# Softmax sums of the row mixing: four reciprocals replaced by a logarithm, an exponential and one correcting step

## The reference, cut to what matters

```
def _L0_xattn_ref(q, k, v, gamma):
    h = N_HEAD                         # 8 heads of 32 rows in each of 8 batches
    qk = jnp.einsum('bhdq,bhdl->bhql', qh, kh) * scale
    sm = jax.nn.softmax(qk, axis=-1)
    ret = jnp.einsum('bhql,bhdl->bhdq', sm, vh)
    ...
    return gamma * ret
x = x + _L0_xattn_ref(_layernorm(x), ctx_2048, ctx_2048, L0_xattn_gamma)
```

## Time and profile before

| what | value |
| --- | --- |
| median of three runs | 1866.02 us |
| profiled execution | 1868.98 us, span 1867.2 us |
| PE busy over the span | 91% |
| DVE, ACT, POOL busy over the span | 80%, 67%, 49% |
| row mixing | from the start to about 361 us of the span |
| one step with unpacking | 19.83 us |
| one step without unpacking | 19.60 us |

### The profile page before, as it was taken

How to read it: one execution, slowest core, us unless ns; L and a number is a source line. 1 busy time by engine, 2 the same in 40 slices (tenths; PEclk the granted TensorE clock), 3 DMA queues, 4 the chain that set the end, 5 groups by cost and what they waited for, 6 DMA issues and landing times. The chain is left out here.

```text
span 1867.2 us, 30272 instructions
## 1 busy us (share of the span) xinstructions
PE 1699.0 (91%) x10553; PEld 747.7 (40%) x10706; DVE 1494.4 (80%) x2799; ACT 1248.7 (67%) x2107; POOL 907.1 (49%) x927
## 2 busy tenths in 40 slices
PE   3999999689999977989799999999999997999999
PEld 0333233134444433434244444444444444444444
DVE  5899999876867664877699999999999995884332
ACT  4888888445544431223399999999999995774333
POOL 5667665355445420000088888888888884000000
PEclk8999999889999998999899999999999998999999
DMA  9856551301011005556455555655666667110220
GB/s 203 224 147 139 143 145 29 105 11 23 1 23 23 1 6 175 101 101 116 89 108 108 109 109 108 113 109 114 114 114 106 105 108 229 31 23 27 42 45 23
DMA packets 421687, 170.45 MB, mean 91 GB/s; under 512 B 382112, under 2 KB 392352, under 8 KB 420384
## 3 DMA queue, kind: packets, MB, share of 16 engines
q1 hardware_dynamic: 421536, 168.51, 41.8%
HBM read 69.89 MB, written 4.19 MB: 40 GB/s over the span
## 5 line engine op out<-in xcount | busy, mean ns | idle before, releaser
L1586 ACT ACTIVATE a_prob<-a_psS,a_bias,q_scale 128x1024 uint8<-128x1024 f32 x512 | 610.7, 1210 | 25.5 <-PE a_psS L1479 20.5
L1515 DVE TENSOR_REDUCE a_tops<-a_psM 128x1 f32<-128x512 f32 x1024 | 622.7, 681 | 2.0 <-PE a_psM L1469 0.6
L1565 POOL CAST a_wide<-a_pairs 128x2048 int16<-128x2048 uint8 x256 | 481.4, 1891 | 96.9 <-DMA a_pairs<-a_prob 87.8
L1469 PE MATMUL a_psM<-KT,QO 128*128 128x512 bf16 x969 | 354.0, 387 | 21.9 <-DVE a_tops L1515 10.5
L1479 PE MATMUL a_psS<-KT,QO 128*128 128x512 bf16 x966 | 292.6, 380 | 6.7 <-ACT a_prob L1586 3.7
L1491 PEld LDWEIGHTS a_psO<-V,a_wide 128*128 128x128 f16 x4096 | 174.9, 96 | 144.9 <-DVE QO L1528 23.0
L1491 PE MATMUL a_psO<-V,a_wide 128*128 128x32 bf16 x4096 | 181.3, 177 | 20.4 <-DVE QO L1528 15.6
L843 DVE SCALAR_TENSOR_TENSOR g_sum<-g_psG,gu_scale,g_sum 128x512 f32<-128x512 f32 x176 | 124.2, 746 | 89.8 <-PE g_psG L995 75.0
L821 POOL TENSOR_TENSOR g_sum<-g_sum 128x512 f32<-128x512 f32 x88 | 126.3, 1435 | 140.4 <-DVE g_sum L843 140.4
L478 ACT ACTIVATE prob<-psT 128x512 f32<-128x512 f32 x256 | 142.9, 599 | 63.8 <-remote 32.0
L942 ACT ACTIVATE g_sum<-g_psG,gu_scale 128x512 f32<-128x512 f32 x176 | 111.2, 681 | 109.9 <-PE g_psG L995 109.0
(11 more groups left out here) (212 smaller groups left out, 2737.5 us busy)
## 6 DMA issues: line engine op xcount, KB each, us to landing
xs<-in_x SPq DMA_DIRECT2D x64, 256.0 KB, 6.2
cs<-in_ctx SPq DMA_DIRECT2D x64, 256.0 KB, 8.3
KT<-in_w SPq DMA_DIRECT2D x2, 4096.0 KB, 19.1
raw_gu<-in_gu SPq DMA_DIRECT2D x4, 1408.0 KB, 8.1
vs<-in_ctxT SPq DMA_DIRECT2D x16, 256.0 KB, 2.9
QO<-in_ctxT SPq DMA_DIRECT2D x4, 1024.0 KB, 11.3
a_pairs<-a_prob SPq DMA_TRANSPOSE x256, 2.7
out<-x_sb SPq DMA_DIRECT2D x16, 256.0 KB, 2.2
```

Of the source, the lines that this page charges most:

```text
L1469: pe.matmul(psM[n % NM][:, :], QOf[:, i * P:(i + 1) * P], KTf[:, keys:keys + 512], start=True, stop=True).then_inc(shown, 1)
L1515: v.reduce_max(tops[i // JOIN % NB][:, i % JOIN, c:c + 1], psM[n % NM][:, :], AX.X).then_inc(topped, 1)
L1565: pool.tensor_copy(wide[i % NV][:, :, :, :].rearrange("p k c q -> p k (c q)"), both).then_inc(widened, 1)
L1586: act.activation(prob[i % NP][:, k * HK:(k + 1) * HK], psS[g % NS][:, :], ACT.Exp, scale=q_scale[:, i:i + 1], bias=bias[i // JOIN % NB][:, ...
```

## The change

The four reciprocals of 128 columns on VectorE go. In their place ScalarE computes the logarithm of the sums straight from PSUM and then the exponential of its negative, which gives an approximate reciprocal r of the whole 512 columns. One correcting step follows: with the sum s, r is improved to r(2 - s r). VectorE computes -s r into e_sums (scalar_tensor_tensor), and then (2 - s r) times weighed (a second scalar_tensor_tensor); GpSimd's product with r is what it was. ScalarE's four instructions of `collect` are spread over n = 0, 1, 2 and 4, where the two of before stood at n = 0. VectorE's two stand at n = 8 and 11, where its four stood at 5, 8, 11 and 14. TensorE's weighed sums of the next tile wait for three reads of psO and psE, where they waited for two.

```diff
-    INVERT, STATS = (5, 8, 11, 14), (2, 13)
+    COLLECT, INVERT, STATS = (0, 1, 2, 4), (8, 11), (2, 13)
@@ GpSimd, finish(j)
-                pool.wait_ge(inverted, HT * (j + 1))
-                pool.tensor_tensor(weighed[j % 2][:, :], weighed[j % 2][:, :], rinv[:, :],
+                pool.wait_ge(inverted, j + 1)
+                pool.tensor_tensor(weighed[j % 2][:, :], weighed[j % 2][:, :], rinv[j % 2][:, :],
@@ ScalarE
-            def collect(j):
+            def collect(j, i):
...
-                act.activation(weighed[b][:, :], psO[:, :], ACT.Copy, scale=gamma[:, :]).then_inc(o_read, 1)
-                act.activation(e_sums[b][:, :], psE[:, :], ACT.Copy).then_inc(o_read, 1)
+                if i == 0:
...
+                    act.activation(weighed[b][:, :], psO[:, :], ACT.Copy, scale=gamma[:, :]).then_inc(o_read, 1)
+                if i == 1:
+                    act.activation(e_sums[b][:, :], psE[:, :], ACT.Copy).then_inc(o_read, 1)
+                if i == 2:
+                    if j:
+                        act.wait_ge(rinv_ready, j)
+                    act.activation(logs[:, :], psE[:, :], ACT.Ln).then_inc(o_read, 1)
+                if i == 3:
+                    act.wait_ge(o_read, 3 * (j + 1))
+                    act.activation(rinv[b][:, :], logs[:, :], ACT.Exp, scale=-1.0).then_inc(rinv_ready, 1)
@@ VectorE
-            def invert(j, h):
...
-                at = slice(h * P, (h + 1) * P)
-                v.reciprocal(rinv[:, at], e_sums[j % 2][:, at]).then_inc(inverted, 1)
+            def invert(j, i):
+                b = j % 2
+                if i == 0:
+                    v.wait_ge(rinv_ready, j + 1)
+                    v.scalar_tensor_tensor(out=e_sums[b][:, :], in0=e_sums[b][:, :], scalar=-1.0, in1=rinv[b][:, :],
+                                           op0=ALU.mult, op1=ALU.mult).then_inc(corrected, 1)
+                if i == 1:
+                    v.wait_ge(corrected, j + 1)
+                    v.scalar_tensor_tensor(out=weighed[b][:, :], in0=e_sums[b][:, :], scalar=2.0,
+                                           in1=weighed[b][:, :], op0=ALU.add, op1=ALU.mult).then_inc(inverted, 1)
@@ TensorE, weigh(j, 0)
-                        pe.wait_ge(o_read, 2 * j)
+                        pe.wait_ge(o_read, 3 * j)
```

More of the change, by code:

```diff
@@ L260, in mix_rows @@
         e_sums = [sb(f"e_sums{i}", [P, DM], F32) for i in range(2)]
-        rinv = sb("rinv", [P, DM], F32)
+        logs = sb("logs", [P, DM], F32)
+        rinv = [sb(f"rinv{i}", [P, DM], F32) for i in range(2)]
         psS = [pb(f"psS{i}", [P, DM], F32) for i in range(3)]
@@ L275, in mix_rows @@
         tscored, exped, pv_done, o_read = (sem(f"m_{n}") for n in ("tscored", "exped", "pv_done", "o_read"))
+        rinv_ready, corrected = sem("m_rinv"), sem("m_corrected")
         inverted, mixed_s, added, after_s, bits_s = (
@@ L479, in exp @@
                                scale=float(D0) ** -0.5).then_inc(exped, 1)
-            def collect(j):
+            def collect(j, i):
                 b = j % 2
[L484 to L487, removed]
-                act.activation(weighed[b][:, :], psO[:, :], ACT.Copy, scale=gamma[:, :]).then_inc(o_read, 1)
-                act.activation(e_sums[b][:, :], psE[:, :], ACT.Copy).then_inc(o_read, 1)
+                if i == 0:
+                    act.wait_ge(pv_done, NU * (j + 1))
+                    if j >= 2:
+                        act.wait_ge(mixed_s, j - 1)
+                        act.wait_ge(added, j - 1)
+                    act.activation(weighed[b][:, :], psO[:, :], ACT.Copy, scale=gamma[:, :]).then_inc(o_read, 1)
[8 more added lines that the diff above has]
+                    act.activation(rinv[b][:, :], logs[:, :], ACT.Exp, scale=-1.0).then_inc(rinv_ready, 1)
             def first_high(k):
@@ L501, in steps @@
                         exp(j, n)
-                    if n == 0 and has(j - 1):
-                        collect(j - 1)
+                    if n in COLLECT and has(j - 1):
+                        collect(j - 1, COLLECT.index(n))
                     if has(j + 2):
@@ L517, in _ @@
             turns(steps)
-            collect(NT - 1)
+            for i in range(len(COLLECT)):
+                collect(NT - 1, i)
         @block.vector
@@ L654, in _ @@
             turns(steps)
-            for h in range(HT):
-                invert(NT - 1, h)
+            for i in range(len(INVERT)):
+                invert(NT - 1, i)
             after(NT - 2)
```

## The result

The changed kernel takes 1871.68 us (median of 9 runs, 1869.71 to 1873.92), the kernel before 1865.41 us in the same comparison (9 runs, 1863.23 to 1867.11). The ratio is 1.0033, 95% interval 1.0023 to 1.0043: slower by 0.33%, or 6.3 us, although VectorE (DVE) has less to do: 1477.3 us busy instead of 1494.4. ScalarE (ACT) rose from 1248.7 to 1264.2. The profiled execution took 1871.7 us, with a span of 1869.9 us and a mean granted clock of 0.98.

The account below looks back on a forecast made before the run. PE's own work plus three short waits for DVE bound a step. Steps 3 to 13 +6.6, steps 1 and 2 +0.8, step 14 -0.26, step 15 +0.4, tail -2.65: +4.9, giving 1870.9 us; range 1867 to 1876.

Parts of the forecast that it names:

- Of the reciprocals only the one at n = 8 counts at the sixteenth score: PE's wait for the sixteenth score: one of four removed reciprocals counts, gaining 0.26 us if its replacement starts on time.
- The first new instruction is held by the keys: DVE's first scalar_tensor_tensor waits for GpSimd's keys until 10.7; sixteenth score at 12.0 instead of 11.86, 0.14 us lost.
- Queries later, unpacking and second new instruction held, split late: GpSimd's queries start at 12.7 and delay DVE; PE's turning of the maxima at 16.7, 0.6 us a step lost.
- Which hold costs how much: Steps with unpacking: DVE's new instructions wait for GpSimd's keys and queries, losing 0.6 us a step.
- Steps 1 and 2 at +0.4 each: Row mixing steps without unpacking: turning of the maxima at 16.25 instead of 15.86, together +0.8 us.
- Step 13 counted as one more of 0.6: Last of steps 3 to 13, each taken to lose 0.6 us, 11 times, +6.6 us.
- Step 14 at -0.26: Row mixing step in which GpSimd makes no keys or queries: 0.26 us gained.
- Step 15 at +0.4: Row mixing step without scores: the logarithm stands in the chain of exponentials PE follows, 0.4 us lost.
- tail at -2.65: End of the row mixing: the shorter chain starts GpSimd's last product at 355.15 instead of 357.81, 2.65 us gained.
- not held: Rival: DVE's new instructions never wait for GpSimd; 0.46 us gained in 11 steps, together -8.1, 1857.9; chance 0.17.
- only the first hold: Rival: only DVE's first new instruction waits for GpSimd; 0.0 a step, tail gain remains, -2, 1864; chance 0.17.
- ScalarE takes over: Rival: logarithm and exponential cost 0.8 each, delaying exponentials and queries; 0.3 a step more, +9, 1875; chance 0.08.

Follow-up runs that it names:

- Experiment 3: Kernel before with its four reciprocals kept; ScalarE's logarithm and exponential added as in the changed kernel, result unused: 1869.39 us, ratio 1.001 to the kernel before.
- Experiment 4: Changed kernel with the second scalar_tensor_tensor moved behind the split (n = 14), the first left at n = 8: 1863.33 us, ratio 0.9978 to the kernel before.
- experiment 1: Changed kernel with both scalar_tensor_tensor replaced by one-input statistics instructions, correcting step left out: 1862.68 us, ratio 0.9971 to the kernel before.

## Why the prediction held, step by step

It said 1870.9 and slower by 4.9 us; the medians say 1871.7 and 6.3. That the two times lie within 0.8 is in part luck: the change was 1.4 larger than the sum, and the kernel before 0.6 faster in the second comparison (1865.41 against 1866.02).

- *Of the reciprocals only the one at n = 8 counts at the sixteenth score.* Held for the one at n = 5: the three maxima behind it start at 8.42 in both profiles, and in the changed one DVE sits idle 0.93 ahead of them (210.70). DVE's busy time in the window of 200 to 220 us fell from 19.63 to 18.04, and the step got longer. The one at n = 11 stood right ahead of the split, so it did lie on PE's path, by at most the wait of 0.17 there; the working has it in the instants, but not in that sentence.
- *The first new instruction is held by the keys.* Held: keys to 10.74 (10.7 said), instruction 1.07 long (about 1.1 said), score at 12.04 (12.0). PE's wait there grew from 0.81 to 0.99 (near 0.9 said).
- *Queries later, unpacking and second new instruction held, split late.* Held: queries at 12.77 (12.7), turning at 16.67 (16.7), so 0.6 a step against 0.57 measured. The cut of the queries came at 11.45, within the 11.4 to 11.5 said; an idle time of 0.5 can't take up the 0.6 that the working has it take, a slip of 0.1. Two sizes were off. The second instruction was 1.04 long, not 1.2, and PE's wait ahead of the turning 0.56, not 0.8. By the working's own instants the wait was 16.7 less 16.0; I had set the turning's delay of 0.6 on top of 0.17 instead, without taking off what the sixteenth score itself had come later.
- *Which hold costs how much.* The working laid the loss on the holds of the new instructions. Experiment 3 shows that it is not theirs alone: with reciprocals in their places the later queries cost 0.40 a step by themselves, through the unpacking instruction. Experiment 4 shows in turn that with the second moved away 0.61 is saved although the queries are as late, and experiment 1 that 0.67 is saved with both unheld. The two can't be added, since the reciprocals fill more of DVE's time ahead of the split than the new instructions do unheld. No run has the new instructions in their places with the queries as early as before, so how the 0.57 divides is open.
- *Steps 1 and 2 at +0.4 each.* Measured +0.38.
- *Step 13 counted as one more of 0.6.* Mis-sized: +1.11. Before the change this step was 19.29, not 19.83; I had multiplied one step's row without reading the last of them. With the 0.5 of step 14 this makes up the 0.9 by which the row mixing's +5.8 exceeds the +4.9; the other differences cancel.
- *Step 14 at -0.26.* Wrong in sign, +0.23. I had GpSimd down as free there, since it makes no keys or queries. But the second new instruction itself releases GpSimd's product, which then holds a cast of the split. Timelines of DVE, POOL and PE in step 14:
```profile
337.82 0.68 DVE L590 SCALAR_TENSOR_TENSOR weighed<-e_sums,weighed 128x512 f32<-128x512 f32 x1
...
338.84 1.14 DVE L568 CAST rparts<-rrest 128x16 bf16<-128x16 f32 x1
```
```profile
338.64 1.29 POOL L414 TENSOR_TENSOR weighed<-weighed,rinv 128x512 f32<-128x512 f32 x1 [10.78 <-DVE weighed L590]
```
```profile
340.24 0.24 PE L726 MATMUL psS<-id_b,rparts 128*51 128x128 bf16 x1 [0.36 <-DVE rparts L569]
```
- *Step 15 at +0.4, tail at -2.65.* Measured +0.48 and -2.58.

The rivals: "not held" falls by the 1.07 and 1.04 of the profile; "only the first hold" is what experiment 4 makes, with its step (19.8) and its gain, and isn't what this kernel does. "ScalarE takes over" falls, as PE waits for a maximum and the split, and for no `prob` in a step with unpacking; its logarithm and exponential are 0.63 long each, not 0.8. Its remark that the queries come later too was the part that experiment 3 confirms.

Not settled is how the 6.3 us of the medians divide beyond the 5.8 of the row mixing: 0.5 is within what the interval allows.

## What to carry to other kernels

Work taken off the busiest engine counts only where another engine waits for it: 2.2 us less a step on DVE (an estimate from the pitches) was a loss here, since most of the reciprocals' time had lain beside PE's own work. When a one-input DVE instruction is replaced by one with two SBUF inputs, mark on the timeline where GpSimd runs, and where the two meet let it end 0.55 us after GpSimd does (of its own 0.68 it had done next to nothing until then); then put it into a stretch where GpSimd is still and PE has work (here behind the split), which turned a loss of 5.8 us in the row mixing into a gain of 7.8, and of 9.0 with ScalarE's part moved as well (by the ratios, a loss of 0.3% into gains of 0.6% and 0.8%). An engine that nobody waits for can still cost by what it delays: its later output moves a GpSimd instruction onto a DVE one.

## What the runs showed of the hardware that I had not expected

A hold needn't go away with the instruction that suffered it: with the new ones unheld, a cast of 17 columns, 0.11 to 0.17 long otherwise, took 1.06 in experiment 1, one of 16 columns 1.14 in step 14.

The time that PE takes to come back to the full clock after it has been idle differs between executions of the same code. In a later stage, whose code is the same, PE waits for a transfer and then does 32 matmuls; after a second idle time it does 8 more. The windows are those of these 32 and 8 (columns: window, length, busy time of PE, PEld, DVE, ACT, POOL, granted clock, DMA share, GB/s), before and after:
```profile
705.58:722.52 16.94, 16.94 (x32) 7.08 (x32) 5.34 (x8) 2.06 (x3) 0.00 (x0) 0.82 0.95 341
727.64:733.48 5.84, 5.83 (x8) 2.45 (x10) 0.00 (x0) 0.00 (x0) 0.00 (x0) 0.63 0.00 0
```
```profile
710.06:725.97 15.91, 15.91 (x32) 6.79 (x32) 5.34 (x8) 2.06 (x3) 0.00 (x0) 0.88 1.03 381
731.10:736.42 5.32, 5.32 (x8) 2.31 (x10) 0.00 (x0) 0.00 (x0) 0.00 (x0) 0.69 0.00 0
```
The granted clock is 0.82 and then 0.63 in one, 0.88 and 0.69 in the other, and the same matmuls take 1.0 and 0.5 us less. The wait for the transfer (`QO` from `in_ctxT`) differs as well, 18.0 us before and 16.8 after.

From the end of the last matmul ahead of that wait to the first of the stage behind (`a_psM`) it is 227.1 us before and 227.0 in experiment 4, but 223.1 to 224.1 after and in the other five. Of the 3.0 between before and after the wait for the transfer makes 1.2, and the matmuls at a lower clock most of the rest. The kernel's change doesn't sort these runs, since experiment 4 goes with the kernel before. So the spans of two profiled executions can differ by 3 us in code that wasn't changed, and differences of this size are read from steps, and with care from medians.
